# A chain between two attention stages regrouped by token halves, and a block loop written out

## What is computed

```python
x = x + cross_attention(layernorm(x), ctx, mask)   # 16 heads of 32
x = x + latent_attention(layernorm(x))             # 16 heads of 128 + 64, causal
x = x + experts(layernorm(x))                      # top 8 of 48 kept
```

```python
# end of the cross-attention
ctx = probs @ v / denominators                     # per head
delta = rs * (ctx @ Wo.T + bo)
x = x + (delta - mean) / sqrt(var + 1e-5) * gamma + beta
# start of the latent attention, h = layernorm(x)
cq  = rms_norm(h @ w_qa.T)                         # 384 wide
ckv = h @ w_kva.T                                  # 128 latent, 64 positions
k_pe = ckv[..., 128:] * cos + rotate_half(ckv[..., 128:]) * sin
ckv_l = rms_norm(ckv[..., :128])
q, kv = cq @ w_qb.T, ckv_l @ w_kvb.T
```

## Time and profile before

| | before |
|---|---|
| median of 3 runs | 815.14 us |
| profiled execution: time | 816.73 us |
| profiled execution: span | 815.2 us, 17046 instructions |
| mean granted clock | 0.964 |
| TensorE busy | 745.8 us (91%) |
| VectorE busy | 603.9 us (74%) |
| ScalarE busy | 410.8 us (50%) |

### The profile page before, as it was taken

The page is one execution under the profiler, slowest core; times in us unless marked ns, Lnnn a source line. Parts: engine busy times, 40 slices in busy tenths (PEclk is TensorE's granted clock), DMA queues, the critical chain, the costliest instruction groups (busy, mean ns, idle before and its releaser), DMA issues.

```text
span 815.2 us, 17046 instructions
## 1 busy us (share of the span) xinstructions
PE 745.8 (91%) x6810; PEld 462.5 (57%) x6810; DVE 603.9 (74%) x955; ACT 410.8 (50%) x536; POOL 8.3 (1%) x27
## 2 busy tenths in 40 slices
PE   8999999899999998647799994699999999999997
PEld 3544444344444444324577762567777777777774
DVE  4598888588888875343588885478888888888885
ACT  3567667466766667201366662334444444444442
POOL 2000000000000000000000000000000000000000
PEclk9999999899999999978799997799999999999999
DMA  9811010101000100031033400087777777777770
GB/s 311 299 54 53 2 54 2 55 2 53 2 2 2 54 1 2 27 155 51 1 117 116 154 26 0 15 270 234 231 231 235 239 236 230 231 237 233 243 230 27
DMA packets 30358, 96.13 MB, mean 118 GB/s; under 512 B 6065, under 2 KB 15713, under 8 KB 28001
## 3 DMA queue, kind: packets, MB, share of 16 engines
q1 hardware_dynamic: 30016, 95.33, 35.4%
q10 hardware_dynamic: 288, 0.02, 0.0%
HBM read 94.73 MB, written 0.57 MB: 117 GB/s over the span
## 4 chain that ended last, share of the span: by engine, by line
PE 71%; issue 20%; DVE 5%; ACT 3%; POOL 1%; DMA 1%; DVEq 0%; POOLq 0%; SPq 0%; ACTq 0%
PE pS L924 32%; PE pP L924 23%; PE pO L924 8%; PE pD L924 8%; ACT arena L453 2%; DVE xT L685 1%; PE pS L936 1%; DVE xn L616 0%; DVE arena L622 0%; DVE bn L608 0%; DMA arena<-w_scratch 0%; ACT xT L389 0%; DVE arena L711 0%; DMA w_scratch<-arena 0%; DVE x_sb L728 0%
## 5 line engine op out<-in xcount | busy, mean ns | idle before, releaser
L924 PE MATMUL pS<-arena 128*128 128x256 f16 (+2 forms) x2194 | 271.0, 281 | 7.5 <-DVE arena L718 3.7
L924 PEld LDWEIGHTS pS<-arena 128*128 128x128 f16 (+1 forms) x2194 | 222.5, 103 | 60.7 <-issue 11.1
L924 PE MATMUL pP<-arena 128*128 128x512 f16 x960 | 234.6, 384 | 3.1 <-DVE arena L622 3.1
L924 PEld LDWEIGHTS pP<-arena 128*128 128x128 f16 x960 | 90.2, 99 | 127.8 <-issue 26.9
L453 ACT ACTIVATE arena<-pS,mblk 128x1024 f32<-128x1024 f32 x128 | 147.2, 1200 | 18.9 <-PE pS L924 15.7
L673 DVE TENSOR_SCALAR arena<-arena 128x1024 f32<-128x1024 f32 x128 | 88.4, 693 | 55.0 <-ACT arena L453 51.6
L837 DVE SCALAR_TENSOR_TENSOR arena<-arena 128x1536 f16<-128x1536 f32 x72 | 126.1, 1751 | 2.4 <-ACT arena L550 2.4
L567 ACT ACTIVATE arena<-pS 128x256 f32<-128x256 f32 x72 | 27.6, 383 | 163.9 <-PE pS L924 163.9
L550 ACT ACTIVATE arena<-arena 128x1536 f16<-128x1536 f32 x72 | 106.3, 1477 | 0.2 <-DMA arena<-in_units 0.2
L924 PE MATMUL pO<-arena 128*32 128x256 f32 (+5 forms) x1264 | 97.5, 368 | 5.8 <-DVE arena L797 3.1
L924 PE MATMUL pD<-arena 128*128 128x512 f16 x288 | 76.5, 379 | 6.5 <-DVE arena L899 5.0
(11 more groups left out here) (171 smaller groups left out, 496.5 us busy)
## 6 DMA issues: line engine op xcount, KB each, us to landing
arena<-in_units SPq DMA_DIRECT2D x72, 768.0 KB, 4.9
arena<-w_scratch SPq DMA_DIRECT2D x144, 64.0 KB, 2.7
mw_in<-in_mla_in SPq DMA_DIRECT2D x8, 1024.0 KB, 6.8
arena<-in_ctxT SPq DMA_DIRECT2D x7, 1024.0 KB, 6.6
mw_out<-in_mla_out SPq DMA_DIRECT2D x8, 512.0 KB, 3.5
arena<-in_wkT SPq DMA_DIRECT2D x4, 256.0 KB, 4.4
arena<-in_ctxT SPq DMA_DIRECT2D x4, 256.0 KB, 5.0
arena<-in_wqT SPq DMA_DIRECT2D x1, 1024.0 KB, 8.1
```

The costliest lines, as they stand in the source:

```text
L924: return pe.matmul(o, lhsT, rhs, start=start, stop=stop, **kw)
```

## The change

The loop over blocks 1 to 4 is written out on TensorE, ScalarE and VectorE. In block 7 the denominators of the first two head groups are read after step 3's values, inverted, spread and applied inside the block, and the output products of these two groups begin there. What is left of the chain goes by token halves: reciprocals, spreading, multiplication, output product, normalisations, transposes, latent products, squares and scales. The closing zero products are gone; the last products of each sum carry the stop. `rs` is folded into `gamma`, and its square into the variance. `wqaT` and `wkvaT` become one array `wlatT`, so that a half's latent products are four of 512 columns. The six table ops of VectorE, and two small new ones, move ahead of block 7; the splits of the first pair's weights move into block 6. Twenty products of zeros (`keep_warm`) follow the output product. The norm's weights are applied while the high and low parts are made, straight from PSUM. Three DMAs (`cosT`, `sinT`, `gateT`) move to the start of SP's list, behind a wait for the split value weights. The opening zero products of the latent attention move behind its first pair's projections.

SP and GpSimd:

```diff
                 load_mla_out(m, m)
+            sp.wait_ge(s["wk_lo"], 2 * HC)
+            sp.dma_start(cosT, a["cosT"]).then_inc(s["rope_in"], 16)
+            sp.dma_start(sinT, a["sinT"]).then_inc(s["rope_in"], 16)
+            sp.dma_start(gateT, a["gateT"]).then_inc(s["gate_in"], 16)
...
-            sp.wait_ge(s["x_acc_done"], 1)
-            sp.dma_start(cosT, a["cosT"]).then_inc(s["rope_in"], 16)
-            sp.dma_start(sinT, a["sinT"]).then_inc(s["rope_in"], 16)
-            sp.dma_start(gateT, a["gateT"]).then_inc(s["gate_in"], 16)
...
+            for k in range(2 * TT):
+                t = slice(k % TT, k % TT + 1)
+                pool.wait_ge(s["var_ready"], k + 2)
+                pool.tensor_tensor(rstd[:, t], var[:, t], nhalf[:, 0:1], ALU.pow).then_inc(s["rstd_ready"], 1)
+            for t in range(TT):
+                pool.wait_ge(s["lvar_ready"], t + 1)
+                pool.tensor_tensor(lrs[:, t], ssq[:, t], nhalf[:, :], ALU.pow).then_inc(s["lrstd_ready"], 1)
```

ScalarE:

```diff
+                    if b == NBLK - 2 and i == HC:
+                        split_q(0, 0)
+                        split_kv(0, 0)
+                    if last and i == 6:
+                        act.wait_ge(s["denb_done"], 1)
+                        act.activation(rden[:, 0:2], pP[:, :].rearrange("p (g q) -> p g q", g=2), ACT.Copy)\
+                           .then_inc(s["rden_ready"], 1)
+
+            for b in range(NBLK - 2):
+                x_block(b, b % 2)
...
+            x_block(NBLK - 1, 1, proj=False, split=False, last=True)
+
+            for t in range(TT):
+                act.wait_ge(s["denb_done"], t + 2)
+                act.activation(rden[:, 2:4, 128 * t:128 * t + 128], pS[:, t, 0:256].rearrange("p (g q) -> p g q", g=2),
+                               ACT.Copy).then_inc(s["rden_ready"], 1)
+            for t in range(TT):
+                act.wait_ge(s["tr_done"], t + 2)
+                act.activation(xT[:, :, 128 * t:128 * t + 128], pS[:, t, :].rearrange("p (c q) -> p c q", c=HC), ACT.Copy)\
+                   .then_inc(s["xT_ready"], 1)
+            for t in range(TT):
+                act.wait_ge(s["lat_mm"], t + 1)
+                act.activation(cqn[:, t], pS[:, 2 + t, 0:QLR], ACT.Square, scale=float(QLR) ** -0.5,
+                               accum_out=ssq[:, t, 0:1])
+                act.activation(kvn[:, t], pS[:, 2 + t, QLR:QLR + KVLR], ACT.Square, scale=float(KVLR) ** -0.5,
+                               accum_out=ssq[:, t, 1:2]).then_inc(s["ssq_ready"], 1)
...
+            act.wait_ge(s["lat_tr"], 1)
             for c in range(QC + 1):
-                act.wait_ge(s["lat_ready"], c + 1)
-                act.activation(lath[:, c], lat[:, c], ACT.Copy, scale=SA).then_inc(s["lat_hi"], 1)
+                act.activation(lath[:, c], lat_ps[c], ACT.Identity, scale=lnw[:, c:c + 1]).then_inc(s["lat_hi"], 1)
```

VectorE:

```diff
+                    if b == NBLK - 2 and i == HC + 1:
+                        split_q(0, 0)
+                        split_kv(0, 0)
+                    if last and i == 4:
+
+                        dve.wait_ge(s["pv_done"], PAIRS_X * b + 4)
+                        dve.tensor_scalar(den, pD[:, 0:T], 1e-30, None, ALU.max).then_inc(s["den_read"], 1)
+                        dve.wait_ge(s["den_read"], 1)
+                        dve.reciprocal(rd[:, 0], den).then_inc(s["den_ready"], 1)
+                    if last and i == 6:
+                        dve.wait_ge(s["rden_ready"], 1)
+                        link(dve.tensor_tensor(ctxn[:, 0:2], pO[:, 0, :].rearrange("p (g q) -> p g q", g=2), rden[:, 0:2],
+                                               ALU.mult))
+                        for c in range(2):
+                            done = dve.tensor_scalar(ctxn[:, c], ctxn[:, c], xb[:, 2, c:c + 1], None, ALU.add)
+                        done.then_inc(s["ctxn_ready"], 1)
...
             link(dve.tensor_scalar(rs[:, :], rs[:, :], 0.0, 0.3, ALU.max, ALU.min))
-            dve.tensor_scalar(bo_b[:, :], bo_b[:, :], rs[:, 0:1], None, ALU.mult)
+            dve.tensor_tensor(rs2[:, :], rs[:, :], rs[:, :], ALU.mult)
+            dve.tensor_scalar(gam_b[:, :], gam_b[:, :], rs[:, 0:1], None, ALU.mult)
+            dve.tensor_scalar(lnw[:, :], lnw[:, :], SA, None, ALU.mult)
             for t in range(TT):
                 last = dve.tensor_tensor(x_sb[:, t, :], x_sb[:, t, :], bet_b[:, :], ALU.add)
             link(last)
...
             link(dve.tensor_copy(o2n_f, o2n_r[:, :]))
             link(dve.tensor_scalar(keep, o2n_f, -1.0, None, ALU.not_equal))
             link(dve.tensor_scalar(nkeep, keep, 1.0, -NEG, ALU.subtract, ALU.mult))
             link(dve.tensor_copy(o2n_cf, o2n_c[:, :]))
             link(dve.tensor_copy(iota_f, iota_i[:, :]))
             link(dve.tensor_scalar(emap, iota_f, o2n_cf, None, ALU.is_equal))
+            x_block(NBLK - 1, 1, proj=False, split=False, last=True)
+
+            dve.wait_ge(s["pv_done"], PAIRS_X * NBLK)
+            link(dve.tensor_scalar(den, pD[:, 0:T], 1e-30, None, ALU.max))
+            for t in range(TT):
+                cols = slice(128 * t, 128 * t + 128)
+                dve.reciprocal(rd[:, 1, cols], den[:, cols]).then_inc(s["den_ready"], 1)
+            for t in range(TT):
+                cols = slice(128 * t, 128 * t + 128)
+                dve.wait_ge(s["rden_ready"], t + 2)
+                link(dve.tensor_tensor(ctxn[:, 2:4, cols], pO[:, 1, :].rearrange("p (g q) -> p g q", g=2)[:, :, cols],
+                                       rden[:, 2:4, cols], ALU.mult))
+                for g in range(2, 4):
+                    last = dve.tensor_scalar(ctxn[:, g, cols], ctxn[:, g, cols], xb[:, 2, g:g + 1], None, ALU.add)
+                last.then_inc(s["ctxn_ready"], 1)
...
+            for t in range(TT):
+                dve.wait_ge(s["delta_done"], t + 1)
+                link(dve.tensor_tensor(work[:, t, :], d_ps[t], bo_b[:, :], ALU.add))
+                half_stats(work, t)
+                dve.tensor_scalar(var[:, t:t + 1], mv[:, t, 1:2], rs2[:, 0:1], 1e-5, ALU.mult, ALU.add)\
+                   .then_inc(s["var_ready"], 1)
+            for t in range(TT):
+                link(dve.scalar_tensor_tensor(work[:, t, :], work[:, t, :], mv[:, t, 0:1], gam_b[:, :],
+                                              ALU.subtract, ALU.mult))
+                dve.wait_ge(s["rstd_ready"], t + 2)
+                link(dve.scalar_tensor_tensor(x1_sb[:, t, :], work[:, t, :], rstd[:, t:t + 1], x_sb[:, t, :],
+                                              ALU.mult, ALU.add))
+                half_stats(x1_sb, t)
+                dve.tensor_scalar(var[:, t:t + 1], mv[:, t, 1:2], 1e-5, None, ALU.add).then_inc(s["var_ready"], 1)
+            for t in range(TT):
+                dve.wait_ge(s["rstd_ready"], t + 2 + TT)
+                dve.tensor_scalar(xn[:, t, :], x1_sb[:, t, :], mv[:, t, 0:1], rstd[:, t:t + 1],
+                                  ALU.subtract, ALU.mult).then_inc(s["xn_ready"], 1)
...
+            for t in range(TT):
+                dve.wait_ge(s["ssq_ready"], t + 1)
+                dve.tensor_scalar(ssq[:, t], ssq[:, t], 1e-6, None, ALU.add).then_inc(s["lvar_ready"], 1)
+                dve.wait_ge(s["lrstd_ready"], t + 1)
+                dve.tensor_scalar(cqn[:, t], pS[:, 2 + t, 0:QLR], lrs[:, t, 0:1], None, ALU.mult)
+                dve.tensor_scalar(kvn[:, t], pS[:, 2 + t, QLR:QLR + KVLR], lrs[:, t, 1:2], None, ALU.mult)\
+                   .then_inc(s["latn_ready"], 1)
```

TensorE:

```diff
-                if with_sums:
+                                  v_sb[:, p, tile, 128 * g + 32 * j:128 * g + 32 * j + 32], probs[:, tile, j, :], False,
+                                  last_block and tile == CT - 1, skip_group_check=True)
+                if last_block:
+                    if i == 4:
+                        pe.wait_ge(s["den_read"], 1)
                     for tile in (2 * (i % 2), 2 * (i % 2) + 1):
                         for j in range(4):
-                            last = mm(pD[32 * j:32 * j + 32, 0:T], onecol[:, g, :], probs[:, tile, j, :], False, False,
-                                      skip_group_check=True)
+                            last = mm(pD[32 * j:32 * j + 32, 0:T], onecol[:, g, :], probs[:, tile, j, :], False,
+                                      i == PAIRS_X - 1 and tile == CT - 1, skip_group_check=True)
...
+            def out_rows(t, gs):
+
+                for g in gs:
+                    done = mm(d_ps[t], ctxn[:, g, 128 * t:128 * t + 128], woT[:, g, :], g == 0, g == HC - 1)
+                return done
...
+                    if last and i == 6:
+                        pe.wait_ge(s["zc_ready"], 1)
+                        pe.wait_ge(s["den_ready"], 1)
+                        for g in range(2):
+                            done = mm(pP[:, T * g:T * g + T], selrow[:, g, :], rd[:, 0], True, True)
+                        done.then_inc(s["denb_done"], 1)
+                    if last and i == 7:
```

(56 more changed lines are left out.)

188 lines of the change are left out of this document (52 added, 136 removed).

## The result

| | before | after |
|---|---|---|
| median of the runs (lowest to highest) | 814.62 us (813.37 to 816.29, 4 runs) | 794.17 us (793.51 to 794.82, 4 runs) |
| profiled execution | 816.7 us | 793.51 us |
| span, mean granted clock | 815.2 us, 0.964 | 791.8 us, 0.978 |

The ratio is 0.9757, interval 0.9739 to 0.9775: faster by 20.5 us in the medians and by 23.2 in the two profiled executions. The forecast was 26.2, with 789.0 for the median; 794.17 lies inside the range of 783 to 797.

A forecast was written before the change was run, and what follows sets the result against it. TensorE-bound, with a stall at the loop's return and a waiting chain between stages. Chain -22.3, places 2 and 3 +2.4, loop -6.3: -26.2 us, so 790.5 profiled and 789 for the median, range 783 to 797.

The forecast's parts named there:

- The mechanism: Chain from denominators to first pair's scores: early and halved work cuts 64.7 us to 42.4, a gain of 22.3.
- The rotation: VectorE's position-key rotation before the first query product: ready last, at 31.1 us after the denominators, other branch at 29.9.
- Step 1, the loop: Cross-attention loop over blocks 1 to 4: writing it out removes the return's stall and slow clock, -6.3 us.
- 12% rival that the stall stays: Block loop: the stall isn't removed but recurs once in the straight code, 795 us; 12%.
- starving straight code: Straight code of eight blocks on TensorE outruns its instruction supply at boundaries, 6.3 us per stall, 820 us; 3%.
- Step 2, work ahead of block 7: VectorE's table ops and two tiny ones between blocks 6 and 7 delay the first clips: +1.8 us, bounds 0 and 2.2.
- Step 3, early denominators: Block 7: broadcasts and output products of the first head groups placed inside the block cost +0.6 us.
- Step 4, extra instructions by halves: Chain after the denominators: each extra instruction from halving costs 0.14 us, four on the path, 0.55.
- one fall, worth 2.9: First half's transposes and latent products: clock falls to 1.2 GHz behind 3.9 us idle, +2.9 us, bounds 0 and 3.9.
- Gaps are 2.6 at most elsewhere: Rest of the chain to the first scores: TensorE's idle gaps at most 2.6 us, so no further fall expected.
- rival of longer hand-overs (793): Chain: some 20 more semaphore hops and one more slow stretch before the first pair, 793 us; 12%.
- 25% rival, that the clock stays up with these fillers: Latent products and first pair: clock stays at 2.4 GHz as fillers shorten the idle, 786 us; 25%.

The follow-up runs named there:

- e11: e10 with VectorE's low parts of the latents moved ahead of the last three rotation operations: 785.47 us, ratio 0.9649 to the kernel before.
- e8: The changed kernel without the early denominators, all four head groups after block 7, still by token halves: 796.73 us, ratio 0.9784 to the kernel before.
- e9: The kernel before, unchanged, profiled once more: 815.64 us (one run).
- e1: The kernel before with only its loop over blocks 1 to 4 written out on TensorE, ScalarE and VectorE: 810.99 us, ratio 0.9965 to the kernel before.
- e3: The changed kernel with blocks 3 and 4 in a loop of a single turn on TensorE: 793.43 us, ratio 0.9726 to the kernel before.
- e2: The changed kernel with the loop over blocks 1 to 4 put back on TensorE alone: 797.51 us, ratio 0.9788 to the kernel before.
- e4: The changed kernel with VectorE's six table operations moved back behind xn: 791.19 us, ratio 0.9700 to the kernel before.
- e5: The changed kernel with seven products of zeros on TensorE in block 7's first step: 791.64 us, ratio 0.9725 to the kernel before.
- e7: The changed kernel with 34 instead of 20 products of zeros behind the output product: 789.52 us, ratio 0.9696 to the kernel before.
- e10: The changed kernel with tables back behind xn, 34 fillers, four zeros behind latent transposes, nine before first pair's scores: 785.57 us, ratio 0.9646 to the kernel before.
- e6: The changed kernel without the twenty products of zeros behind the output product: 792.58 us, ratio 0.9749 to the kernel before.

## Why the prediction was right and where it was wrong

**The mechanism held.** The chain between the stages gave 21.55 us of the 22.3 forecast. The milestones, after the denominators: second delta 7.6 (forecast 7.2), first transposes 15.2 and end of the second `xn` 16.05 (first and second `xn`: 15.4 and 16.2), first query product 33.0 (34.0), first scores 43.2 (42.4). The rotation was indeed late last, and e11 shows it by an edit. Without the early part the chain still takes 16.2 us less than before (e8: 48.56 from the denominators to the first pair's scores). How that divides between the halves, the joined weight array, the folded scale and the rest isn't shown: no run takes them out one by one. The weights' splits in block 6 cost nothing: from block 6's context product to block 7's scores of step 1 it is 38.91 us in both traces.

**Step 1, the loop: right in the pair of traces, mis-sized for the median.** In the traces it gave 6.1 for 6.3. But the term was read from one execution whose clock had fallen behind the stall; with the clock kept the stall is 3.1 (e9), and the median gain is 3.3 (e1). The forecast corrected for the profiled execution as a whole (1.6 us above the median) but not for the term that carried the excess. If 3.3 is the usual price, that is about 3 of the 5.2 us by which the median missed; with e1's interval of 0.9 to 4.9 this is an estimate and not shown. The 12% rival that the stall stays was wrong (e1, e3), and so was starving straight code: no boundary has a gap. The Trainium skill (Runtime: NRT & Kernel Launch, section Instruction fetch mechanics) says that a taken branch to a page that isn't held stalls while crossings in straight code are mostly hidden. e2 against e3 agrees: 4.6 us with the jump, 0 without.

**Step 2, work ahead of block 7: the delay right, the clock left out.** Forecast 1.8, measured 2.9, above the upper bound of 2.2. The delay itself is 1.5 (e4). The other 1.3 is that TensorE, idle for 1.41 and then 1.69 us, goes to 1.2 GHz (granted 0.61 over 306.3 to 310), shown by e5. The step priced the wait and not what a second idle close to a first does to the clock.

**Step 3, early denominators: right.** 0.7 for 0.6, and e8 shows what they earn. The forecast had no term of its own for that gain.

**Step 4, extra instructions by halves: over-priced.** Each was put at 0.14 us, four of them 0.55. The two halves of the reciprocal take 1.76 us, the whole took 1.75; the first bias adds of 128 columns start 0.20 apart where adds of 256 in the same trace start 0.34 apart (0.065 per extra one); only the multiply costs 0.19 (0.46 from start to start for 256 columns, 0.73 for 512). Together some 0.33. The forecast let the row decide against the Trainium skill (VectorE: DVE Perf Modes, section on the TRN2 errata), by which the four were an estimated 0.24. That took 58 cycles for each; the same table of the Trainium skill has 120 for an operand out of PSUM, as the multiply's is, so an estimated 0.31 for the four. The trace lies near to that: one operation's price isn't another's.

**The clock: right that it falls, wrong in where and how often.** The forecast had one fall, worth 2.9, before the first scores. In the profiled execution it fell only after the transposes (0.63 us, near full clock), worth 1.7 in the latent products. It fell again in the first pair's projections, another 1.7 (7.12 for 5.45), and in pair 0's first scores (2.65 for 1.96 us). "Gaps are 2.6 at most elsewhere" was taken as safe from one row (2.40 us before 338.11); falls behind 1.69 and 1.90 us are what failed it, and behind that very 2.40 us in the kernel before itself (e9). One execution had the clock up there and another did not: the row was no ground for safety. Without the two falls the query product would stand at 31.3 and the scores 8.56 behind it, forecast 31.1 and 8.4: the hops were counted well, so the rival of longer hand-overs (793) was right only in its further slow stretch. The 25% rival, that the clock stays up with these fillers, was wrong; e7 and e10 show what it took here, zeros until just before the product that waits.

**The tail: a term nobody priced.** Behind the first scores the changed kernel loses 0.65. The largest piece is the round trip through `w_scratch`: from the issue of the transfer to it until the product that needs what comes back it is 7.25 us (500.16 to 507.41) against 6.26 before (524.34 to 530.60), because the read back is issued 2.48 us after the write instead of 1.64. Over the thirteen traces of this case, alike at that place, the time runs from 6.22 to 7.29 us, and 7.29 is in e1, which has the chain of before. So this is scatter of that transfer from execution to execution, and no effect of the change that could be shown. What sets it wasn't tried.

**The balance.** In the traces 2.8 us were missed: loop 0.2, step 2 1.1, step 3 0.1, chain 0.75, tail 0.65. The medians gained 20.5 us, 5.7 less than forecast: what is not in the 2.8 is, within 0.1, that the profiled execution of before lay 2.1 us above its median and that of after 0.7 below. Since the median of before itself came out 0.5 us lower than it stood in the forecast, 789.0 was missed by 5.2.

## What to carry to other kernels

Read a stall in at least two executions before pricing it, and split it into the idle and what the clock does behind it: here one and the same return cost 3.1 us once and 6.3 once, and one and the same idle time left the clock up once and not the next time. When work is moved ahead of a latency-bound step, price the clock as well as the wait; and when TensorE is to be kept at full speed over a wait, let the zeros reach close to the waiting product: twenty of them, which left 3.44 us, brought nothing that could be shown, thirty-four, which left 0.42, brought 2.2 against none. What lies between wasn't tried.

## What the runs showed that was not expected

A taken jump back over two blocks of TensorE code costs 3.1 to 6.3 us, a loop of the same form without the jump 0 (e3). TensorE fell to 1.2 GHz behind idles of 1.69 us (after 1.41 just before) and 1.90 us, yet kept 2.4 GHz behind the same 1.90 us in e6 and e7, and behind 2.67 us in e6; behind 2.40 us the kernel before kept it in one execution and lost it in another (e9): what the length of one idle does isn't fixed by the length alone. The same is seen far behind the change, in the products ahead of `w_scratch`, in the changed kernel and then in e4:

```profile
499.05 3.36 PE L947 MATMUL pS<-arena 128*48 128x256 f32 x26 [0.52 <-DVE arena L908]
```

```profile
497.20 5.03 PE L947 MATMUL pS<-arena 128*48 128x256 f32 x26 [0.52 <-DVE arena L908]
```

The last long idle ahead of them was 1.64 us in the one and 1.66 in the other. Nine zeros before the first pair's scores, which themselves wait for VectorE, shorten nothing. The scores behind them ran at full clock (1.96 us in e10 and e11), but so they did in e6 without them (2.45 us in e7), so what the nine are worth isn't shown.
